# A gated graph network on one core: slices in three units, 14 blocks a step, one branch, dense products across layers

## The reference

```python
h = jnp.maximum(_layernorm(x, axis=-1), 0.0)
h = h @ lin_w.T + lin_b
for i in range(3):
    m = h @ weight[i]
    agg = jax.ops.segment_sum(m[src], dst, num_segments=n_nodes)
    h = gru_cell(agg, h, w_ih, w_hh, b_ih, b_hh)
return x + h
```

## Time and profile before

| | |
|---|---|
| median of three runs | 5499.25 us (5487.53 to 5519.9) |
| the profiled execution | 5490.06 us, span 5488.0 us |
| instructions | 75039 |
| granted TensorE clock, mean | 0.794 |
| HBM | 790 MB read, 250 MB written |

### The profile page before, as it was taken

The page is one execution under the profiler, slowest core; times in us unless marked ns, Lnnn a source line. Parts: engine busy times, 40 slices in busy tenths (PEclk is TensorE's granted clock), DMA queues, the critical chain, the costliest instruction groups (busy, mean ns, idle before and its releaser), DMA issues.

```text
span 5488.0 us, 75039 instructions
## 1 busy us (share of the span) xinstructions
PE 3593.0 (65%) x24940; PEld 2923.5 (53%) x24941; DVE 2878.7 (52%) x8384; ACT 2541.4 (46%) x2819; POOL 3358.8 (61%) x3230
## 2 busy tenths in 40 slices
PE   5256666666666667774777666676746767776776
PEld 3144444444444455663666665566635656665665
DVE  7244545544555445552555555555535555555555
ACT  4144444444444445542455555455434544444443
POOL 4655556566556566655666666566656656666665
PEclk8577777777777778886878888788868888888888
DMA  7465666666666676674666666566745656665664
GB/s 239 134 167 166 174 173 181 175 175 177 175 177 179 169 252 201 201 227 139 205 204 203 204 199 209 180 221 206 226 154 194 210 183 203 193 208 186 203 201 151
DMA packets 795433, 1046.01 MB, mean 191 GB/s; under 512 B 91672, under 2 KB 669592, under 8 KB 795032
## 3 DMA queue, kind: packets, MB, share of 16 engines
q1 hardware_dynamic: 527720, 652.21, 36.5%
q0 software_dynamic: 152064, 311.63, 21.4%
q10 hardware_dynamic: 115248, 77.10, 4.5%
HBM read 790.11 MB, written 250.48 MB: 190 GB/s over the span
## 4 chain that ended last, share of the span: by engine, by line
PE 37%; issue 19%; another core or an unknown queue 16%; DVE 16%; ACT 9%; DVEq 1%; DMA 1%; POOL 1%; ACTq 1%; SPq 0%; POOLq 0%
PE psum L834 15%; PE psum L815 12%; ACT wide_counts L655 7%; PE psum L798 3%; DVE message_halves L1249 3%; DVE onehot L1113 3%; DVE message_halves L1251 3%; PE psum L786 2%; DVE messages_region L1212 1%; ACT messages_region L679 1%; DVE aggT L1137 1%; PE psum L758 1%; PE psum L771 1%; PE psum L759 1%
## 5 line engine op out<-in xcount | busy, mean ns | idle before, releaser
L541 POOL DMA_INDIRECT ring_region<-messages,edge_src x3168 | 3304.8, 1043 | 2031.0 <-issue 1187.8
L834 PE MATMUL psum<-wide_counts,message_halves 128*128 128x432 f32 x7448 | 1864.3, 407 | 934.0 <-issue 359.4
L834 PEld LDWEIGHTS psum<-wide_counts,message_halves 128*128 128x128 f32 x7448 | 1565.7, 216 | 1133.9 <-issue 780.7
L655 ACT CAST wide_counts<-messages_region 128x3024 fp32r<-128x3024 f16 x532 | 1439.4, 2715 | 1150.8 <-remote 430.2
L815 PE MATMUL psum<-messages_region 128*128 128x238 bf16 (+2 forms) x5376 | 875.6, 323 | 558.9 <-issue 399.2
L679 ACT CAST messages_region<-psum 128x504 f16<-128x504 f32 x1344 | 732.0, 585 | 738.3 <-remote 345.9
L815 PEld LDWEIGHTS psum<-messages_region 128*128 128x128 bf16 x5376 | 573.6, 118 | 846.3 <-issue 652.8
L1249 DVE CAST message_halves<-messages_region 128x896 fp32r<-128x896 f32 x532 | 574.8, 1080 | 466.5 <-remote 217.1
L1137 DVE TENSOR_TENSOR aggT<-aggT,psum 128x36 f32 x792 | 152.0, 192 | 1097.3 <-remote 704.0
L1251 DVE TENSOR_TENSOR message_halves<-messages_region,message_halves 128x896 fp32r<-128x896 f32 x532 | 581.3, 1093 | 18.4
L798 PE MATMUL psum<-onehot,ring_region 128*128 128x36 bf16 x9504 | 352.6, 186 | 221.0 <-issue 151.2
(11 more groups left out here) (104 smaller groups left out, 1667.6 us busy)
## 6 DMA issues: line engine op xcount, KB each, us to landing
messages_region<-counts SPq DMA_DIRECT2D x532, 768.0 KB
counts<-messages_region SPq DMA_DIRECT2D x1344, 128.0 KB
ring_region<-messages,edge_src POOLq DMA_INDIRECT x3168
messages_region<-plain SPq DMA_DIRECT2D x28, 896.0 KB
messages<-pieces_out ACTq DMA_DIRECT2D x98, 192.0 KB
temps<-states ACTq DMA_DIRECT2D x98, 128.0 KB
states<-temps ACTq DMA_DIRECT2D x98, 128.0 KB
plain<-temps ACTq DMA_DIRECT2D x98, 128.0 KB
```

What stands on the lines that cost most here:

```text
L541: nc.gpsimd.indirect_dma_start(out=rows[:, n % RING, h * QC + c, :], out_offset=None, in_=messages[layer], in_offset=bass.IndirectOffsetOn ...
L655: nc.scalar.copy(wide_counts[:, v % UBUF, :, :], stage[v % ABUF][:, :, 0:HB * W]).then_inc(s_wide, 1)
L834: mm = nc.tensor.matmul(psum[:, 6 + kg % 2, 0:DQ * W], halves[:, v % UBUF, b % HB, half * P:(half + 1) * P], wide_counts[:, v % UBUF, :, c ...
```

## The change

- `UNITS = ((0, 2), (2, 4), (4, 7))`: a slice is widened and split in three units, of 2, 2 and 3 blocks, each with its own count in `s_dense`, `s_wide`, `s_high` and `s_low`. Loads stay whole slices. A unit is made in the step in which the unit two slices before is used (`units_and_sums`).
- 14 blocks in each step (`STEP_BLOCKS`), so that superblocks end with a step. `dense_blocks(True)` lets the list run on: the five tail steps of layer 0 have blocks of layer 1, the last five steps of layer 1 have blocks of layer 2, and the last five steps of layer 2 have none. A superblock of layers 1 and 2 is summed five steps earlier, and the tiles' steps are worked out anew from that.
- ScalarE makes a step's units after the middle piece. VectorE makes all units of a step ahead of the superblock's adds.
- The one-hot of a step is one instruction of 128 x 288 with two broadcast inputs.
- One flag, `general`, is tested once in each engine's program; the usual path has no other branch. The general path has the tiles and extra windows after each layer.
- SP loads the parts of the whole messages between the slices, and the loads ahead of the counting are gone.

```diff
-EARLY = (2, 4, 4)
+UNITS = ((0, 2), (2, 4), (4, 7))
+UN = len(UNITS)
+LEAD = 5
+TAIL_SPARE = 4
...
-LOW_LAG = (3, 2, 2)
...
-            free = s + TILE_SPACING[layer]
+            free = s + (TILE_SPACING[layer] if s < DENSE_FROM[layer] else 1)
...
+    def units_and_sums(blocks_at, ahead):
+        left, done, summed, order = {}, {}, {}, []
+        for where, blocks in sorted(blocks_at.items()):
+            for d in blocks:
+                v, b = d // HB, d % HB
+                for j, (_, last) in enumerate(UNITS):
+                    if b == last - 1:
+                        done[UN * v + j] = where
+                if d % NB == NB - 1:
+                    summed[d // NB] = where
+        for w in range(UN * SLICES * (DENSE0[-1] + NSB)):
+            where = done[w - UBUF * UN] if w >= UBUF * UN else (0, TURN - 1)
...
-            prologue_scratch_free(sp)
-            for i in range(PARTS):
-                messages_in(0, i)
...
+            def widen(w):
+                v = w // UN
+                cols = slice(*(W * b for b in UNITS[w % UN]))
+                if w % UN == 0:
+                    act.wait_ge(s_al[v % ABUF], 16 * (v // ABUF + 1))
+                unit_used(act, w - UBUF * UN)
+                nc.scalar.copy(wide_counts[:, v % UBUF, :, cols], stage[v % ABUF][:, :, cols]).then_inc(s_wide, 1)
...
-                for h, q in enumerate(quads_of(layer, s)):
-                    for c in range(QC):
-                        made = nc.vector.tensor_scalar(onehot[:, n % 3, h * QC + c, :], iota_lo[:, 0:W],
-                                                       edge_rel[:, q * QC + c:q * QC + c + 1], None, ALU.is_equal)
-                made.then_inc(s_oh, 1)
+                first = quads_of(layer, s)[0]
+                nc.vector.tensor_tensor(
+                    onehot[:, n % 3, :, :], iota_lo[:, 0:W].unsqueeze(1).to_broadcast([P, 2 * QC, W]),
+                    edge_rel[:, first * QC:(first + 2) * QC].unsqueeze(2).to_broadcast([P, 2 * QC, W]), ALU.is_equal
+                ).then_inc(s_oh, 1)
...
-                    for v in SLICES_AT_TAIL.get((layer, s), ()):
-                        while ended and (DENSE0[layer] + ended[0] + 1) * SLICES <= v:
+                    ended = [kg for kg, where in summed.items() if where == (layer, s)]
+                    for w in units.get((layer, s), ()):
+                        while ended and UN * SLICES * (ended[0] + 1) <= w - UBUF * UN:
                             add_superblock(layer, ended.pop(0), s)
-                        split(layer, v)
+                        split(w)
...
+            with dve.If(general < 1):
+                for layer in range(LAYERS):
+                    layer_steps(layer, TILES_AT[layer], AHEAD)
+            dve.end_ifs()
```

More of the change, by code:

```diff
@@ L152, in ready_after @@
         begun = DENSE_FROM[layer] + i * GSB
-        return max(begun - 1 if offset < DQ else begun + (offset - DQ) // 2, superblock_step(layer, i))
+        dense = begun + GSB - 1 - (LEAD if layer else 0)
+        return max(begun - 1 if offset < DQ else begun + (offset - DQ) // 2, dense)
     def schedule(layer):
@@ new lines, in dense_blocks @@
+    def dense_blocks(ahead):
+        at, d = {}, 0
+        ends = [NB * (DENSE0[layer] + len(DENSE_OF[layer])) for layer in range(LAYERS)]
+        for layer in range(LAYERS):
+            for s in all_steps(layer, TILES_AT[layer]):
+                end = ends[layer]
+                if s < DENSE_FROM[layer]:
+                    continue
+                if ahead and layer < LAYERS - 1:
+                    step_of = {t: step for step, t in TILES_AT[layer].items()}
+                    for i in range(PARTS - 1):
+                        if s < step_of[min(NT, 2 * HB * P * (i + 2) // TN) - 1] + TAIL_SPARE:
+                            break
+                        end = ends[layer] + 2 * HB * (i + 1)
+                elif s >= STEPS[layer]:
+                    break
+                now = min(d + STEP_BLOCKS, max(d, end))
+                at[layer, s] = range(d, now)
+                d = now
+        assert d == ends[-1]
+        return at
@@ new lines, in units_and_sums @@
+    def units_and_sums(blocks_at, ahead):
[10 more added lines that the diff above has]
+            where = done[w - UBUF * UN] if w >= UBUF * UN else (0, TURN - 1)
+            layer = max(l for l in range(LAYERS) if DENSE0[l] <= w // (UN * SLICES))
+            if layer and not ahead:
+                where = max(where, (layer, 0))
+            left.setdefault(where, []).append(w)
+        return left, summed
@@ L170, in added, with dense_done @@
+    AHEAD, BEHIND = dense_blocks(True), dense_blocks(False)
+    for layer in range(LAYERS):
+        for s, t in TILES_AT[layer].items():
+            last = min(NQ, int(bound(t)) + 1) - 1
+            kg = DENSE0[layer] + last // SQ - DENSE_OF[layer][0]
+            assert last // SQ < DENSE_OF[layer][0] or units_and_sums(AHEAD, True)[1][kg] < (layer, s)
     def added(layer, s):
         return 2 * (STEP0[layer] + min(s, STEPS[layer]))
-    def dense_done(layer, s):
-        done = sum(1 for i in range(len(DENSE_OF[layer])) if superblock_step(layer, i) < s)
-        return DQ * (DENSE0[layer] + done)
+    def dense_done(summed, layer, s):
+        return DQ * sum(1 for where in summed.values() if where < (layer, s))
@@ L872, in _, with layer_steps @@
             pe.wait_ge(s_flags, 1)
-            wide = flag_value(mybir.EngineType.PE, 0)
-            late = flag_value(mybir.EngineType.PE, 1)
-            def layer_steps(layer, tiles_at):
+            general = flag_value(mybir.EngineType.PE, 1)
+            def layer_steps(layer, tiles_at, blocks_at, wide=None):
+                _, summed = units_and_sums(blocks_at, wide is None)
                 for s in all_steps(layer, tiles_at):
                     n = STEP0[layer] + s
+                    if wide is not None and s == STEPS[layer]:
+                        extra_windows(layer, wide)
                     if s < STEPS[layer]:
@@ L1242, in split @@
-            def split(layer, v):
+                if low_tile(layer, tiles_at, s, 2) is not None:
+                    low_piece(layer, low_tile(layer, tiles_at, s, 2))
+            def split(w):
+                v = w // UN
                 used, j = v // SLICES, v % SLICES
-                if used == DENSE0[layer] and j % 2 == 0:
-                    dve.wait_ge(s_res[j // 2], 16 * (layer + 2))
-                slice_used(dve, v - UBUF)
-                whole = res[:, HB * j:HB * (j + 1), :]
-                high, low = (halves[:, v % UBUF, :, half * P:(half + 1) * P] for half in range(HALVES))
+                layer = max(l for l in range(LAYERS) if DENSE0[l] <= used)
+                first, last = UNITS[w % UN]
+                if used == DENSE0[layer] and j % 2 == 0 and w % UN == 0:
+                    dve.wait_ge(s_res[j // 2], 16 * (layer + 1))
+                unit_used(dve, w - UBUF * UN)
+                whole = res[:, HB * j + first:HB * j + last, :]
+                high, low = (halves[:, v % UBUF, first:last, half * P:(half + 1) * P] for half in range(HALVES))
```

242 lines of the change are left out of this document (95 added, 147 removed).

## The result

The changed kernel takes 5298.45 us (median of four runs, 5281.18 to 5317.69) beside 5507.62 for the kernel before: ratio 0.9625, 95% interval 0.9569 to 0.968. It is faster by 3.75%, 209 us; I had forecast 406 us. In the fences, L549 is the gather, L808 the sums, L841 the dense products, L666, L1255 and L1257 the units, L1119 the one-hot, L1144 and L1158 the adds of a step and a superblock.

The account below looks back on a forecast made before the run. No engine is full, so hand-overs between engines bound it. Up to dense work 1883, layer 0 487, tail 70, layer 1 1309 and 34, layer 2 1251 and 48 make 5082; plus 2 and 9, 5093 us; range 4870 to 5440.

Parts of the forecast that it names:

- TensorE's signals arrive late: Dense steps: 43% delayed at 12.4 us, the rest at GpSimd's 10.9; 11.6 us a step taken, for 13.3.
- the late signals set the pace: Rival, dense steps: each needs a pause of the gathers for TensorE's signals, stays near 12.9 us; 5430 us; chance 0.16.
- One-hot: VectorE, every step: eight instructions of 1.22 us become one of 0.46; 30 us of counting's 99 on the path.
- Units: Slices made in three pieces: ScalarE 3.03 us a slice for 2.715, VectorE 2.8 for 2.17; 170 and 335 us added work.
- Order: Dense steps: splits before superblock adds, middle piece before units; VectorE 9.4 us and ScalarE 7.5 lie under GpSimd's 10.9.
- The port: GpSimd's gathers beside VectorE: new one-hot costs at most 0.46 us a step, subtractions grow shorter; nothing added.
- Layer changes: Tail after layer 0 +15 us, to 70; 34 us after layer 1; end of layer 2 48 us for 36.
- Branches: Layer starts: removed branches gain nothing, 10 us each for TensorE's crawl; rival that the branch causes it: 5073 or 5033, chance 0.10.
- Prologue: Start, at 140 us: seven removed loads of whole messages save 20 us, between 0 and 40.
- VectorE's queue as the bound: Rival, dense steps: VectorE's 9.4 us follow each delayed sum; step 13.6 or 14.4 us, 5610 or 5820 us; chance 0.08.
- the general branch: Rival: if taken, tiles come after the layers, 49 x 10 us in each, 1470 in all; 6560 us; chance 0.02.

Follow-up runs that it names:

- e8: Changed kernel with GpSimd issuing a step's second four gathers only when the first four have landed, late chip: 0.9818 of the kernel before, 5387 us.
- e9: Changed kernel with every second gather left out and the remaining chunks multiplied twice, late chip: 0.6865 of the kernel before, 3694.6 us.
- e11: Changed kernel with slices made whole instead of in three units, late chip: 0.962 of the kernel before.
- e18: Changed kernel with whole slices for ScalarE and the signals, only VectorE's split cut in 2, 2 and 3 blocks, late chip: 0.9642 of the kernel before.
- e12: Changed kernel with a step's one-hot made by eight instructions again, late chip: 0.9851 of the kernel before.
- e3: Changed kernel with slices made whole instead of in three units, punctual chip: 0.9835 of the kernel before.
- e14: Changed kernel with the old order (superblock's adds ahead of splits, units ahead of the middle piece), punctual chip: 0.9674 of the kernel before.
- e17: Changed kernel with the old order (superblock's adds ahead of splits, units ahead of the middle piece), late chip: 0.9769 of the kernel before.
- e4: Kernel before with only the one-hot made one instruction, punctual chip: 0.9892 of the kernel before.
- e7: Changed kernel with the tiles that wait for a superblock taken one step later, late chip: 0.9596 of the kernel before.
- e15: Changed kernel with whole slices for ScalarE and the signals, only VectorE's split cut in 2, 2 and 3 blocks, punctual chip: 0.955 of the kernel before.
- e1: Changed kernel run once more as the base, punctual chip: 0.9549 of the kernel before, 4360 us.
- e10: Changed kernel gathering 256 bytes a row for 768, still eight gathers a step, late chip: 0.9669 of the kernel before.
- e2: Changed kernel with a step's one-hot made by eight instructions again, punctual chip: 0.9641 of the kernel before.

## Why the prediction was right or wrong

- **The bound, right in kind, wrong in size.** "TensorE's signals arrive late" is the cause, but the sum took it for 43% of steps at 12.4 and the rest at 10.9, 11.6 us. That is the step that failed. Measured are 12.1 to 12.8 us, 12.6 in the mean, where the rival "the late signals set the pace" had 12.9. The changed kernel has 0.75 to 0.81 pauses of GpSimd in a dense step, 1.9 to 2.2 us together, and a signal passes mostly 1.0 us or more into one, so a shorter chain behind the signal did not bring the step to 10.9: e8 and e9 show that a pause is what lets the signals pass, e11 and e18 that time won at the gathers goes back into the pauses. Why these take 2 us in a dense step and not less stays open. The point that I had given this rival for, that counting took nearly the same 13.8 us with other work, deserved more weight than 0.16. In the terms of the sum (a span of 5280 us for 5082) the three dense stretches took 212 us more than forecast, the layer changes and the end 25 more, and all up to the first dense product 39 less. That counting was mis-sized the other way, and hid part of the miss, was luck.
- **One-hot.** 0.453 us for 0.46 forecast. On the path I took 30 us; in counting on a late chip it is all of it, 124 x 0.76 = 94 us of the 98 measured (e12). I had guessed "a fifth to a third" from no row. By which queue it reaches the path on late chips I haven't shown.
- **Units.** ScalarE's slice went to 2.917 us (3.03 forecast), VectorE's to 2.57 (2.8). That TensorE's idle time before dense products would go was right: 157 us for 934. But most of it goes without the units: with whole slices in the new order it is 1.8 us on the punctual chip (e3) and 214 on a late one (e11), where whole slices cost no time that the intervals show.
- **Order.** It is the part of the dense step's gain that runs show on both kinds of chip (e14, e17), and what pays in it is the middle piece ahead of the units, the loop of the earlier trace rows. The wait of the earlier trace rows is gone too, but not by the order: it does not come back in e14. In e4, the kernel before with the new one-hot on a punctual chip, it stands there 17 times, 8.2 to 8.6 us each. Which of the units and the even 14 blocks took it away isn't shown. The change also brought a wait of its own: gate products for the superblock's adds, 176 us (46.5 before). In e7 it is gone and the time is the same within the intervals, so it was hidden.
- **The port.** "I add nothing" missed a gain: the gather's mean in layer 1 fell from 1.057 to 0.987 us. The Trainium skill (SBUF, Who interferes with whom) would have let each new one-hot hold a gather, 180 us as an estimate. The trace agrees in kind but not in size: the 26 gathers that met the new one-hot and no other VectorE instruction took 1.052 us in the mean, against 0.948 undisturbed and 0.953 beside the old one-hot. What the page says besides, that the one that comes first keeps the shared ports until its instruction ends, agrees with the rows of e3 above, where the gather began 0.28 us after the subtraction and took 1.63 us. Cutting 896 columns into 256, 256 and 384 is worth 130 us there (0.9835 in e3 for 0.955 in e15).
- **Layer changes.** Change after layer 0: +28 us for +15 and 10. After layer 1 37 us for 34. The end took 52 us for 48.
- **Branches.** No run shows a gain of the single branch, as predicted. Layer 1 has no branch ahead of it now, and TensorE still crawls through its first steps, stopping 1 to 3 us between single products:

```profile
2454.23 0.19 PE L808 MATMUL psum<-onehot,ring_region 128*128 128x36 bf16 x1 [3.31 <-issue]
2456.33 0.19 PE L808 MATMUL psum<-onehot,ring_region 128*128 128x36 bf16 x1 [1.91 <-issue]
2459.13 0.19 PE L808 MATMUL psum<-onehot,ring_region 128*128 128x36 bf16 x1 [2.61 <-issue]
```

And e4, which has the branches of the kernel before, does not crawl on its punctual chip at the same place; its first sums of layer 1 are

```profile
1995.53 0.88 PE L798 MATMUL psum<-onehot,ring_region 128*128 128x36 bf16 x24 [21.92 <-DMA ring_region<-messages,edge_src]
```

So the crawl goes with the kind of chip, not with the branch. The Trainium skill (Runtime: NRT & Kernel Launch, Instruction fetch mechanics) says that a taken branch must wait for a fetch when its target lies outside the instructions already held; that doesn't explain stops where no branch is.

- **Prologue.** The first dense product came 88 us earlier; 98 are the counting steps, and the steps before them took 11 us more, so the removed loads show no gain of their own.
- **VectorE's queue as the bound** and **the general branch** didn't occur.

## What to carry to other kernels

When stages with different work take the same time per step, ask what they share before costing the parts, and treat signals that come late as a bound of their own (here the gathers and some 2 us of pauses in a dense step), not as a chance of some steps. The same edit can pay by different mechanisms on different chips, so undo it part by part on the chip where it is timed, and give the number with the kernel before on that same chip. Where the pace of GpSimd's gathers is the bound, one long VectorE subtraction with two inputs in SBUF is worth cutting: 130 us on the punctual chip, nothing measurable on the late ones. And look which of two changes of order brings a wait back before crediting either.

## What the hardware showed that I had not expected

- **Chips differ by 17% on this program.** Before: 5508 us in the first runs, 5480, 5386 and 5473 us on three chips (the first runs' chip is not on record and may be one of them), 4567 and 4564 on two. On the former TensorE's signals are late and TensorE stops 1 to 4 us between products for nothing that the trace shows ("issue" before L808, L823 and L841: 974 us in the changed kernel, none in e1). On the latter neither occurs. Which property of the chip does it, the runs don't tell. The traces differ in one more way: that of the changed kernel keeps 35724 changes of semaphores on the first chip and 104854 on a punctual one (e1), so on late chips most records are missing. Whether the recording itself takes part in delaying the signals there, no run tests. In e9 records are missing as well (45398 kept) and the signals are on time, so the two don't always go together.
- **On such a chip the gathers are what does it.** With four in place of eight a step the lateness was 0.01 us (e9), with a third of the bytes it was 3.56 us (e10), on the same chip.
- **A deliberate pause is nearly free there** (e8, 2%), since a pause is paid for the signals anyway.
- A gather can take 2.75 us beside VectorE's counting one-hots. In the counting steps e2, with eight one-hots a step, has 27 gathers over 2 us and e1 has 2. From e2:

```profile
1009.75 2.75 POOL L549 DMA_INDIRECT ring_region<-messages,edge_src  x1 [0.30 <-issue]
1010.07 2.27 DVE L1219 TENSOR_SCALAR messages_region<-messages_region 128x1176 bf16<-128x1176 f16 x4
```
